# Score and weight blocks of two attention heads: fp32 products on 64 array rows per head in place of split fp32r products on 128 rows, and the second turn of y moved up

## The chip, the cores and the metric

The kernel runs on one core of one Trainium2 chip. The metric is the device time of one execution in microseconds; lower is better. Three executions were timed before the change, and one execution was profiled.

## The reference, cut to what matters

A gated linear attention layer with 64 slots per head, a layer norm, an expert layer and a second layer norm, for 4 batches of 512 tokens of width 512. There are 16 heads. For each head (`q`, `k` 64 wide, `v` 128 wide, `s` 64 slots):

```python
z = cumlogsumexp(s); g = exp(z_prev - z); p = exp(s - z)
hk = hk * g + k_t p_t^T          # step over tokens
ok_t = q_t . hk                  # 64 slots
pv = softmax(ok)
hv = hv * g + p_t v_t^T
ov_t = pv_t . hv                 # 128 wide
o = ov * rsqrt(mean(ov^2) + eps) * g_norm * silu(gate)
out = o @ Wo
```

The kernel computes the recurrences in chunks of 128 tokens. Within a chunk a causal 128x128 block is needed twice for each head: scores (keys times scaled queries, contracted over the head's 64 features), used to sum slots, and weights (the exponentials `e` times `pz`, contracted over the head's 64 slots), used to sum values.

## The kernel before

**Cells.** The attention part is 32 cells: 8 pairs of heads times 4 batches, each with 512 tokens in 4 chunks (`CH`). A cell holds two heads side by side: the 128 partitions of the feature-major tiles `q_t`, `k_t` and `e_t` are 64 rows of one head and 64 rows of the other. The first cell stands ahead of a hardware loop, the loop body has 4 cells, and 3 cells follow it. After the attention comes the expert part (lines from 1091 on), which the change doesn't touch.

**Engines.** The instruction order of each engine is written out by hand, and engines meet at semaphores. TensorE (`cell_tensor`) does, in order: turns (128x128 transposes) of `e` and `k`; the products for v and gate of chunks 0 and 1 (`token_proj`) with the running key sums (`running_keys`); the score blocks; `running_keys(2)`; the turn of `rz`; the turn of half 0 of `y`, the previous cell's output; the slot sums of chunks 0 and 1 into bank `OB`; the turn of half 1 of `y`; the slot sums of chunks 2 and 3; the previous cell's `output_rows`; more v and gate products with `running_values`; the turn of `pz`; the next cell's slot projection; the weight blocks; the next cell's query and key projections; the value products. ScalarE copies banks out and makes the high parts of split numbers, VectorE and GpSimd make the low parts.

**Split products.** A tile is held as high plus low part in type fp32r, and `split_product` (L910) adds three matmuls: high by high, high by low, low by high (L914 to L916). `pair_blocks` (L972) does so for the two blocks of one chunk at once. The left side is the stacked 128 rows of both heads (`lhs_hi`, `lhs_lo`), and the right side is a block-diagonal tile 256 columns wide (`bd_hi`, `bd_lo`), in which each head's 64 rows are filled only in its own 128 columns. Bank `SB[half]` gets chunks 2·half and 2·half+1 of both heads. The parts come from ScalarE (L511, L512, L518, L561, L579, L580), from VectorE (`queries_low` L672, L810 and L812) and from GpSimd (`keys_low` L431, and L445). VectorE then multiplies each bank by the causal mask into `w_t` (`masked`, L683).

**Banks of the turns.** The turned tiles share two PSUM banks, `TB[0]` and `TB[1]`, in the fixed order of L53:

```python
T_USES = ["e", "k", "rz", "y0", "y1", "pz"]
```

They alternate, so `e`, `rz` and `y1` have one bank, and `k`, `y0` and `pz` the other. `turned` (L945) waits, before it writes, until the tile that had the bank before has been read (`wait_read` with `t_read`, L896): `y1` waits for `rz_tok_done`, which ScalarE's copy of the turned `rz` (L558) raises.

Of the kernel before, what the change touches and what calls it, by code (L numbers as in the profile page):

```python
# [11 lines left out]
P = 128  # L12
# [194 lines left out]
def attention(nc, car, x, Wq, Wk, Wv, Wg, Ws, Wo, g_norm, U, V, W1, b1, b2):  # L207
# [10 lines left out]
    with ctx:  # L218
# [26 lines left out]
        bd_hi, bd_lo = sb("bd_hi", [P, 2, T], F32R), sb("bd_lo", [P, 2, T], F32R)  # L245
        lhs_hi, lhs_lo = sb("lhs_hi", [P, T], F32R), sb("lhs_lo", [P, T], F32R)
# [81 lines left out]
        q_lo_done, k_lo_done = sem("q_lo_done"), sem("k_lo_done")  # L328
        e_hi_done, e_lo_done = sem("e_hi_done"), sem("e_lo_done")
# [101 lines left out]
        def keys_low(pool, m):  # L431

            pool.wait_ge(k_done, m.count(1, 1))
            nc.gpsimd.tensor_tensor(lhs_lo[:], k_t[:], lhs_hi[:].bitcast(F32), ALU.subtract).then_inc(k_lo_done, 1)  # L434

        def cell_gpsimd(pool, cell, J=None, last=False):
            if J is not None:

                for i in range(3):
                    split_low(pool, J, i)  # L440
            if last:
                car.norm1_rstd(pool, 0)

            pool.wait_ge(e_hi_done, cell.count(1, 1))
            nc.gpsimd.tensor_tensor(lhs_lo[:], e_t[:, cell.b % 2, :], lhs_hi[:].bitcast(F32),  # L445
                                    ALU.subtract).then_inc(e_lo_done, 1)

            pool.wait_ge(e_tok_hi_done, cell.count(1, 1))
            nc.gpsimd.tensor_tensor(e_tok_lo[:].rearrange("p c (h m) -> p c h m", h=2), e_tok[:, 0:CH - 1, 1:3, :],
                                    e_tok_hi[:].rearrange("p c (h m) -> p c h m", h=2).bitcast(F32),  # L450
                                    ALU.subtract).then_inc(e_tok_lo_done, 1)
            for c in range(CH - 1):
                pool.wait_ge(v_hi_done, cell.count(CH - 1, c + 1))
                nc.gpsimd.tensor_tensor(v_lo[:, c, :], v_tok[:, c, :], v_hi[:, c, :].bitcast(F32),  # L454
                                        ALU.subtract).then_inc(v_lo_done, 1)
            if J is not None:
                for i in range(3, 7):
                    split_low(pool, J, i)
            if not last:
                keys_low(pool, cell.shifted(1))  # L460

            pool.wait_ge(ovar_done, cell.count(1, 1))
            nc.gpsimd.tensor_tensor(orstd[:], ovar[:], minus_half[:], ALU.pow).then_inc(orstd_done, 1)

        @block.gpsimd
        def _(pool):
            pool.wait_ge(own_done, 2)
            nc.gpsimd.affine_select(out=ident[:], in_=ident[:], compare_op=ALU.not_equal, fill=1.0, base=0,
                                    pattern=[[-1, P]], channel_multiplier=1).then_inc(const_done, 1)

            nc.gpsimd.affine_select(out=causal[:], in_=causal[:], compare_op=ALU.is_ge, fill=0.0, base=0,
                                    pattern=[[1, P]], channel_multiplier=-1).then_inc(const_done, 1)
            nc.gpsimd.memset(minus_half[:], -0.5).then_inc(const_done, 1)
            for i in range(7):
                split_low(pool, 0, i)
            pool.wait_ge(const_done, 3)
            keys_low(pool, Cell(None, 0))
            cell_gpsimd(pool, Cell(None, 0))
            with pool.Fori(0, PAIRS - 1) as j:
                for b in range(1, B + 1):  # L480
                    cell_gpsimd(pool, Cell(j, b), j + 1 if b == 3 else None)
            for b in range(1, B):
                cell_gpsimd(pool, Cell(None, B * (PAIRS - 1) + b), last=b == B - 1)
            for kt in range(KT):
                car.w1_low(pool, kt)
# [19 lines left out]
        def queries_scalar(act, m):  # L505
            bk, _ = p_turn(m.shifted(-1), "q")
            ps = PB[bk]
            act.wait_ge(q_proj, m.count(1, 1))
            scale = float(DK) ** -0.5
            nc.scalar.activation(q_t[:], ps[:], ACT.Copy, scale=scale)  # L510
            nc.scalar.activation(bd_hi[0:DK, 0, :], ps[0:DK, :], ACT.Copy, scale=scale)  # L511
            nc.scalar.activation(bd_hi[DK:P, 1, :], ps[DK:P, :], ACT.Copy, scale=scale).then_inc(q_done, 1)  # L512

        def keys_scalar(act, m):
            bk, _ = p_turn(m.shifted(-1), "k")
            act.wait_ge(k_proj, m.count(1, 1))
            nc.scalar.activation(k_t[:], PB[bk][:], ACT.Copy)
            nc.scalar.activation(lhs_hi[:], PB[bk][:], ACT.Copy).then_inc(k_done, 1)  # L518
# [23 lines left out]
        def cell_scalar(act, cell, J=None, wo_J=None, last=False):  # L542
# [17 lines left out]
            act.wait_ge(scores, cell.count(2, 2))  # L560
            nc.scalar.activation(lhs_hi[:], e_t[:, cell.b % 2, :], ACT.Copy).then_inc(e_hi_done, 1)  # L561
# [16 lines left out]
            nc.scalar.activation(pz_t_hi[:].rearrange("p c t -> p (c t)"), TB[bk][:], ACT.Copy)  # L578
            nc.scalar.activation(bd_hi[0:M, 0, :], TB[bk][0:M, :], ACT.Copy)  # L579
            nc.scalar.activation(bd_hi[M:P, 1, :], TB[bk][M:P, :], ACT.Copy).then_inc(pz_t_done, 1)  # L580
# [91 lines left out]
        def queries_low(dve, m):  # L672

            bk, _ = p_turn(m.shifted(-1), "q")
            dve.wait_ge(q_done, m.count(1, 1))
            for h, own_rows in enumerate((slice(0, DK), slice(DK, P))):
                low = nc.vector.scalar_tensor_tensor(out=bd_lo[own_rows, h, :], in0=PB[bk][own_rows, :],
                                                     scalar=float(DK) ** -0.5,
                                                     in1=bd_hi[own_rows, h, :].bitcast(F32), op0=ALU.mult,
                                                     op1=ALU.subtract)  # L680
            low.then_inc(q_lo_done, 1)

        def masked(dve, cell, half, ready, done):  # L683

            dve.wait_ge(ready, cell.count(2, half + 1))
            nc.vector.tensor_tensor(
                w_t[:, 2 * half:2 * half + 2, :, :].rearrange("p c h t -> p (c h) t"),
                SB[half][:].rearrange("p (a t) -> p a t", a=4),
                causal[:].rearrange("p (a t) -> p a t", a=1).broadcast_to([P, 4, P]),
# [56 lines left out]
        def cell_vector(dve, cell, wo_J=None, last=False):  # L746
# [47 lines left out]
            for c in range(CH - 1):  # L794
# [9 lines left out]
                if c == 1:  # L804
# [4 lines left out]
                                            pz_t_hi[:].rearrange("p c t -> p (c t)").bitcast(F32), ALU.subtract)  # L809
                    nc.vector.tensor_tensor(bd_lo[0:M, 0, :], TB[bk][0:M, :], bd_hi[0:M, 0, :].bitcast(F32),  # L810
                                            ALU.subtract)
                    nc.vector.tensor_tensor(bd_lo[M:P, 1, :], TB[bk][M:P, :], bd_hi[M:P, 1, :].bitcast(F32),  # L812
# [15 lines left out]
            if not last:  # L828
                queries_low(dve, nxt)
# [12 lines left out]
        def _(dve):  # L842
# [3 lines left out]
            nc.vector.memset(bd_hi[:].bitcast(F32), 0.0).then_inc(own_done, 1)  # L846
            nc.vector.memset(bd_lo[:].bitcast(F32), 0.0).then_inc(own_done, 1)
            nc.vector.memset(e_tok[:], 0.0).then_inc(own_done, 1)
            dve.wait_ge(own_done, 6)
# [15 lines left out]
            queries_low(dve, m)  # L865
# [6 lines left out]
            dve.wait_ge(own_done, 8)  # L872
# [22 lines left out]
        p_read = {"s": (s_clipped, 1, 2), "q": (q_lo_done, 1, 2), "k": (k_done, 1, 2)}  # L895
# [76 lines left out]
        def pair_blocks(pe, half, done):  # L972

            for c in (2 * half, 2 * half + 1):
                t = tokens(c)
                last = split_product(
                    SB[half][:, (c % 2) * 2 * P:(c % 2 + 1) * 2 * P].rearrange("p (h t) -> p h t", h=2),
                    [((lhs_hi[:, t], lhs_lo[:, t]), (bd_hi[:, :, t], bd_lo[:, :, t]))])
            last.then_inc(done, 1)

        def cell_tensor(pe, cell, last=False):
# [28 lines left out]
            pe.wait_ge(q_lo_done, cell.count(1, 1))  # L1010
            pe.wait_ge(k_lo_done, cell.count(1, 1))
            pair_blocks(pe, 0, scores)
            pair_blocks(pe, 1, scores)
# [3 lines left out]
            if not first(cell):  # L1017
                turned_y(pe, cell, 0)

            for c in range(CH):  # L1020
                if c == 2 and not first(cell):
                    turned_y(pe, cell, 1)
# [4 lines left out]
                pe.wait_ge(scores_masked, cell.count(2, c // 2 + 1))  # L1027
# [36 lines left out]
            pe.wait_ge(pz_lo_done, cell.count(1, 1))  # L1064
            pe.wait_ge(e_lo_done, cell.count(1, 1))
            pair_blocks(pe, 0, weights)
            pair_blocks(pe, 1, weights)
# [9 lines left out]
            for half in range(2):  # L1077
                pe.wait_ge(weights_masked, cell.count(2, half + 1))
# [345 lines left out]
```

## Time and profile before

| what | value |
|---|---|
| median of three timed executions | 1407.0 us (1406.31 to 1410.47) |
| the profiled execution, first to last instruction (span) | 1402.9 us |
| what lies around the span, by the median | 4.1 us |
| TensorE matmul busy | 1370.4 us, 98% |
| VectorE, ScalarE, GpSimd busy | 951.8 us (68%), 567.3 us (40%), 336.4 us (24%) |
| mean granted TensorE clock | 0.998 of full speed |

The profile page gives no execution time of its own beside the span, so the span stands for the profiled execution and 4.1 us is the difference to the median. Matmuls overlap: the time of one in a row is its latency, and what a matmul costs in a stream is the distance from its start to the next one's start. A plain fp32 matmul of the program stands in the trace as two MATMUL records with a weight load (LDWEIGHTS, engine PEld) each. A split product's matmul, or a turn, stands as one.

### The profile page before, as it was taken

What the parts mean: (1) busy time and instruction counts of PE and PEld (TensorE: products, weight loads), DVE (VectorE), ACT (ScalarE), POOL (GpSimd) and SP (SyncE); (2) the same over time, 40 slices, a digit from 0 to 9 for tenths busy, and PEclk for the clock granted to TensorE, in tenths of its full rate; (3) what the DMA queues carried; (4) which work ended last, traced back from release to release, by engine and by line L of the source; (5) the groups of instructions that cost most, each with busy time, mean ns of one, the idle gap of its engine ahead of it and who ended that gap; (6) DMA issues with size and microseconds to landing.
All of it is one profiled execution on the core that took longest, in us unless ns stands there. A gap on an engine that the chain in (4) does not pass through costs nothing. (4 is left out here: it accounts for less than half of the span.)

```text
span 1402.9 us, 21964 instructions
## 1 busy us (share of the span) xinstructions
PE 1370.4 (98%) x7904; PEld 1197.8 (85%) x7904; DVE 951.8 (68%) x1812; ACT 567.3 (40%) x1562; POOL 336.4 (24%) x302
## 2 busy tenths in 40 slices
PE   7999999999999999999999999999999999999998
PEld 6888888888888888888888888888888888878886
DVE  6666776676776677767766776776676767755644
ACT  5344433454344443444334443444344443512210
POOL 3222412233223312331124222331223221210000
PEclk9999999999999999999999999999999999999999
DMA  6000100001000100010001000010000200000000
GB/s 202 9 1 1 51 3 17 0 23 31 16 1 23 30 17 0 2 52 1 16 1 36 17 16 1 23 31 16 1 21 25 61 31 1 1 1 31 30 31 31
DMA packets 35304, 31.78 MB, mean 23 GB/s; under 512 B 7568, under 2 KB 28048, under 8 KB 35216
## 3 DMA queue, kind: packets, MB, share of 16 engines
q1 hardware_dynamic: 35216, 30.44, 7.3%
q8 instruction: 76, 1.25, 0.4%
q14 instruction: 12, 0.10, 0.0%
HBM read 26.24 MB, written 4.19 MB: 22 GB/s over the span
## 5 line engine op out<-in xcount | busy, mean ns | idle before, releaser
L914 PE MATMUL p<-wvg_hi,xt_hi 128*128 128x512 f32 x512 | 210.2, 411 | 0.0
L916 PE MATMUL p<-wvg_hi,xt_lo 128*128 128x512 f32 x512 | 201.2, 393 | 0.0
L915 PE MATMUL p<-wvg_lo,xt_hi 128*128 128x512 f32 x512 | 200.4, 391 | 0.0
L523 ACT ACTIVATE v_tok<-p 128x256 f32<-128x256 f32 x128 | 49.3, 385 | 309.0 <-PE p L916 309.0
L914 PE MATMUL p<-xt_hi,wsqk_hi 128*128 128x512 f32 x384 | 150.5, 392 | 1.4 <-DVE xt_lo L857 1.4
L915 PE MATMUL p<-xt_lo,wsqk_hi 128*128 128x512 f32 x384 | 150.2, 391 | 0.0
L916 PE MATMUL p<-xt_hi,wsqk_lo 128*128 128x512 f32 x384 | 149.4, 389 | 0.0
L454 POOL TENSOR_TENSOR v_lo<-v_tok,v_hi 128x256 fp32r<-128x256 f32 x96 | 84.3, 893 | 195.9 <-ACT v_hi L532 195.9
L434 POOL TENSOR_TENSOR lhs_lo<-k_t,lhs_hi 128x512 fp32r<-128x512 f32 x32 | 41.1, 1284 | 313.3 <-ACT lhs_hi L518 313.3
L916 PEld LDWEIGHTS p<-wvg_hi,xt_lo 128*128 128x128 f32 x512 | 96.3, 188 | 22.5
L915 PEld LDWEIGHTS p<-wvg_lo,xt_hi 128*128 128x128 f32 x512 | 97.0, 190 | 16.7
L914 PEld LDWEIGHTS p<-wvg_hi,xt_hi 128*128 128x128 f32 x512 | 96.8, 189 | 16.2
L670 DVE RECIPROCAL rz_t<-rz_t 128x512 f32<-128x512 f32 x32 | 106.9, 3341 | 0.0
L699 DVE SCALAR_TENSOR_TENSOR gate<-th,p 128x256 f32<-128x256 f32 x128 | 53.9, 421 | 76.0 <-ACT th L527 72.2
L914 PE MATMUL p<-wo_hi,yt_hi 128*128 128x512 f32 x256 | 102.9, 402 | 0.8 <-DVE acc L736 0.5
L916 PE MATMUL p<-wo_hi,yt_lo 128*128 128x512 f32 x256 | 99.9, 390 | 0.0
L915 PE MATMUL p<-wo_lo,yt_hi 128*128 128x512 f32 x256 | 99.7, 389 | 0.0
L445 POOL TENSOR_TENSOR lhs_lo<-e_t,lhs_hi 128x512 fp32r<-128x512 f32 x32 | 40.9, 1277 | 210.4 <-ACT lhs_hi L561 210.4
L736 DVE TENSOR_TENSOR acc<-p,acc 128x512 f32<-128x512 f32 x128 | 87.4, 684 | 1.8 <-PE p L916 1.8
L916 PEld LDWEIGHTS p<-xt_hi,wsqk_lo 128*128 128x128 f32 x384 | 72.1, 188 | 15.5
L914 PEld LDWEIGHTS p<-xt_hi,wsqk_hi 128*128 128x128 f32 x384 | 72.3, 188 | 15.1 <-DVE xt_lo L857 1.8
L915 PEld LDWEIGHTS p<-xt_lo,wsqk_hi 128*128 128x128 f32 x384 | 72.4, 188 | 12.6
(215 smaller groups left out, 3431.1 us busy)
## 6 DMA issues: line engine op xcount, KB each, us to landing
acc<-in_L_attn_hidden_states SPq DMA_DIRECT2D x4, 1024.0 KB, 7.5
raw<-in_L_attn_Wv SPq DMA_DIRECT2D x32, 128.0 KB, 2.4
raw<-in_L_attn_Wg SPq DMA_DIRECT2D x32, 128.0 KB, 2.8
raw<-in_L_attn_Wo SPq DMA_DIRECT2D x16, 256.0 KB, 2.8
out<-acc SPq DMA_DIRECT2D x16, 256.0 KB, 2.3
raw<-in_L_attn_Ws SPq DMA_DIRECT2D x8, 256.0 KB, 2.6
raw<-in_L_attn_Wq SPq DMA_DIRECT2D x8, 256.0 KB, 2.8
raw<-in_L_attn_Wk SPq DMA_DIRECT2D x8, 256.0 KB, 4.6
```

The costliest lines, as they stand in the source:

```text
L434: nc.gpsimd.tensor_tensor(lhs_lo[:], k_t[:], lhs_hi[:].bitcast(F32), ALU.subtract).then_inc(k_lo_done, 1)
L445: nc.gpsimd.tensor_tensor(lhs_lo[:], e_t[:, cell.b % 2, :], lhs_hi[:].bitcast(F32), ALU.subtract).then_inc(e_lo_done, 1)
L454: nc.gpsimd.tensor_tensor(v_lo[:, c, :], v_tok[:, c, :], v_hi[:, c, :].bitcast(F32), ALU.subtract).then_inc(v_lo_done, 1)
L523: nc.scalar.activation(v_tok[:, c, :], PB[bk][:, 0:VW], ACT.Copy).then_inc(v_done, 1)
L670: nc.vector.reciprocal(rz_t[:], rz_t[:]).then_inc(rz_done, 1)
L699: nc.vector.scalar_tensor_tensor(out=gate[:, c, :], in0=th[:, c % 2, :], scalar=1.0, in1=PB[bk][:, VW:2 * VW], op0=ALU.add, op1=ALU.mult). ...
L736: nc.vector.tensor_tensor(a, PB[bk][:], a, ALU.add).then_inc(added, 1)
L914: nc.tensor.matmul(out_, lh, rh, start=(k == 0), stop=False)
L915: nc.tensor.matmul(out_, lh, rl, start=False, stop=False)
L916: last = nc.tensor.matmul(out_, ll, rh, start=False, stop=(k == n - 1))
```

## The change

Both block kinds become plain fp32 products, one per head and chunk, each on its own 64 partitions: rows 0 to 63 for head 0 and 64 to 127 for head 1. Bank `SB[h]` now holds the four chunks of head h, and `head_blocks` goes through the chunks and alternates the heads. All of the `bd` and `lhs` tiles, their copies on ScalarE, their subtractions on VectorE and GpSimd, and two tile clears at the start go. One new fp32 copy of the turned `pz` (`pz_t`) is made ahead of `pz_t_hi`. `masked` handles one head's bank. The slot sums and the value products wait for both masks. The turn of `y` half 1 moves ahead of all slot sums.

```diff
-            act.wait_ge(scores, cell.count(2, 2))
-            nc.scalar.activation(lhs_hi[:], e_t[:, cell.b % 2, :], ACT.Copy).then_inc(e_hi_done, 1)
...
-            nc.scalar.activation(pz_t_hi[:].rearrange("p c t -> p (c t)"), TB[bk][:], ACT.Copy)
-            nc.scalar.activation(bd_hi[0:M, 0, :], TB[bk][0:M, :], ACT.Copy)
-            nc.scalar.activation(bd_hi[M:P, 1, :], TB[bk][M:P, :], ACT.Copy).then_inc(pz_t_done, 1)
+            nc.scalar.activation(pz_t[:], TB[bk][:], ACT.Copy).then_inc(pz_split, 1)
+            nc.scalar.activation(pz_t_hi[:].rearrange("p c t -> p (c t)"), TB[bk][:], ACT.Copy).then_inc(pz_t_done, 1)
...
-        def pair_blocks(pe, half, done):
-
-            for c in (2 * half, 2 * half + 1):
-                t = tokens(c)
-                last = split_product(
-                    SB[half][:, (c % 2) * 2 * P:(c % 2 + 1) * 2 * P].rearrange("p (h t) -> p h t", h=2),
-                    [((lhs_hi[:, t], lhs_lo[:, t]), (bd_hi[:, :, t], bd_lo[:, :, t]))])
-            last.then_inc(done, 1)
+        def head_blocks(keys, queries, done):
+
+            for c in range(CH):
+                t = tokens(c)
+                for h, own_rows in enumerate((slice(0, DK), slice(DK, P))):
+                    mm = nc.tensor.matmul(SB[h][:, t], keys[own_rows, t], queries[own_rows, t],
+                                          start=(c == 0), stop=True, skip_group_check=True)
+                    if c == CH - 1:
+                        mm.then_inc(done, 1)
...
-            pe.wait_ge(q_lo_done, cell.count(1, 1))
-            pe.wait_ge(k_lo_done, cell.count(1, 1))
-            pair_blocks(pe, 0, scores)
-            pair_blocks(pe, 1, scores)
+            head_blocks(k_t, q_t, scores)
...
             if not first(cell):
                 turned_y(pe, cell, 0)
+                turned_y(pe, cell, 1)
 
             for c in range(CH):
-                if c == 2 and not first(cell):
-                    turned_y(pe, cell, 1)
...
-                pe.wait_ge(scores_masked, cell.count(2, c // 2 + 1))
+                pe.wait_ge(scores_masked, cell.count(2, 2))
...
-            pe.wait_ge(pz_lo_done, cell.count(1, 1))
-            pe.wait_ge(e_lo_done, cell.count(1, 1))
-            pair_blocks(pe, 0, weights)
-            pair_blocks(pe, 1, weights)
+            pe.wait_ge(pz_split, cell.count(1, 1))
+            pe.wait_ge(scores_masked, cell.count(2, 2))
+            head_blocks(e, pz_t, weights)
```

The program's instructions for TensorE at the score blocks of a loop cell, before (four groups of three such matmuls stand there; `s` is a bank of `SB`):

```order
L1009 ISA [waits q_done]
L914 MATMUL s<-bd_hi,lhs_hi 128x256 [waits k_lo_done,q_lo_done,y_done]
L915 MATMUL s<-bd_lo,lhs_hi 128x256
L916 MATMUL s<-bd_hi,lhs_lo 128x256
...
L992 REGISTER_ALU
L993 MATMUL xb<-e_tok,k_tok 128x128 [waits hk_kept]
```

The same place now:

```order
L970 ISA [waits q_done]
L937 MATMUL s<-q_t,k_t 128x128 [waits y_done]
L937 MATMUL s<-q_t,k_t 128x128 x7
L953 REGISTER_ALU
L954 MATMUL xb<-e_tok,k_tok 128x128 [waits hk_kept]
```

Twelve matmuls of 256 columns have become eight of 128 columns, and two of the waits are gone.

A few instructions on, TensorE's turns and slot sums, before (`t` is a bank of `TB`, `o` is `OB`):

```order
L950 MATMUL t<-ident,y 128x128 [waits k_tok_done,y_done]
L950 MATMUL t<-ident,y 128x128 x3
L1027 ISA
L1028 MATMUL o<-e_tok,w_t 128x128 [waits scores_masked]
L1030 MATMUL o<-e_tok,w_t 128x128
L1026 MATMUL o<-hk,q_t 128x128 [waits hk_kept]
L1028 MATMUL o<-e_tok,w_t 128x128 [waits scores_masked]
L1030 MATMUL o<-e_tok,w_t 128x128
L950 MATMUL t<-ident,y 128x128 [waits rz_tok_done,y_done]
L950 MATMUL t<-ident,y 128x128 x3
```

and now:

```order
L910 MATMUL t<-ident,rz_t 128x128 x3
L915 REGISTER_ALU
L910 MATMUL t<-ident,y 128x128 [waits k_tok_done,y_done]
L910 MATMUL t<-ident,y 128x128 x3
L910 MATMUL t<-ident,y 128x128 [waits rz_tok_done,y_done]
L910 MATMUL t<-ident,y 128x128 x3
L984 ISA
L985 MATMUL o<-e_tok,w_t 128x128 [waits scores_masked]
L987 MATMUL o<-e_tok,w_t 128x128
```

The turn that waits for `rz_tok_done` stood five slot sums behind the first turn of `y`; now it stands directly behind it.

## Rows read from the trace of the kernel before

**Rows 1.** The page: span, busy time of TensorE and VectorE, granted clock.

```profile
span 1402.9 us, 21964 instructions
PE 1370.4 (98%) x7904; PEld 1197.8 (85%) x7904; DVE 951.8 (68%) x1812; ACT 567.3 (40%) x1562; POOL 336.4 (24%) x302
PEclk9999999999999999999999999999999999999999
```

**Rows 2.** Waits of TensorE: who for whom, us in total, times, longest.

```profile
PE t L950 <- issue: 9.6, 6, 1.8
PE s L1104 <- DMA acc<-in_L_attn_hidden_states: 7.3, 1, 7.3
PE xb L1046 <- POOL v_lo L454: 2.8, 1, 2.8
...
PE s L914 <- DVE bd_lo L812: 0.3, 1, 0.3
```

**Rows 3.** Windows, a cell, its two block passes: us, busy, clock.

```profile
704.49:741.74 37.25, 37.25 (x221) 32.80 (x219) 25.79 (x49) 15.11 (x46) 7.80 (x7) 1.00 0.00 1
710.47:711.88 1.41, 1.41 (x14) 1.41 (x13) 0.93 (x3) 0.66 (x2) 0.00 (x0) 1.00 0.00 0
731.21:732.64 1.43, 1.43 (x13) 1.41 (x12) 0.69 (x1) 0.49 (x1) 0.00 (x0) 1.00 0.00 0
```

**Rows 4.** Timeline from the score blocks to the output rows: start, duration, engine.

```profile
710.47 0.19 PEld L914 LDWEIGHTS s<-bd_hi,lhs_hi 128*128 128x128 f32 x1
...
711.25 0.42 DVE L699 SCALAR_TENSOR_TENSOR gate<-th,p 128x256 f32<-128x256 f32 x1 [0.18 <-ACT th L527]
...
711.58 1.31 DVE L686 TENSOR_TENSOR w_t<-s,causal 128x512 f32<-128x512 f32 x2
...
711.88 0.28 PE L916 MATMUL s<-bd_hi,lhs_lo 128*128 128x256 f32 x1
711.88 0.31 PEld L993 LDWEIGHTS xb<-e_tok,k_tok 128*128 128x128 f32 x2
...
712.12 0.47 PEld L950 LDWEIGHTS t<-ident,rz_t 128*128 128x128 f32 x4
...
712.55 0.47 PEld L950 LDWEIGHTS t<-ident,y 128*128 128x128 f32 x4
...
712.86 0.60 ACT L558 ACTIVATE rz_tok<-t 128x512 f32<-128x512 f32 x1 [1.65 <-PE t L950]
712.99 0.30 PEld L1028 LDWEIGHTS o<-e_tok,w_t 128*128 128x128 f32 x2
713.10 0.39 PE L1028 MATMUL o<-e_tok,w_t 128*128 128x128 f32 x2
713.21 0.30 PEld L1030 LDWEIGHTS o<-e_tok,w_t 128*128 128x128 f32 x2
713.32 0.39 PE L1030 MATMUL o<-e_tok,w_t 128*128 128x128 f32 x2
...
713.87 0.59 ACT L539 ACTIVATE yt_hi<-t 128x512 fp32r<-128x512 f32 x1
...
714.10 0.47 PEld L950 LDWEIGHTS t<-ident,y 128*128 128x128 f32 x4
...
714.50 0.69 DVE L721 TENSOR_TENSOR yt_lo<-t,yt_hi 128x512 fp32r<-128x512 f32 x1 [1.41 <-ACT yt_hi L539]
...
715.88 0.19 PEld L914 LDWEIGHTS p<-wo_hi,yt_hi 128*128 128x128 f32 x1
```

**Rows 5.** Line 558, ScalarE's copy of `rz`: duration min/median/max, first, last; waits.

```profile
L558 ACT ACTIVATE rz_tok<-t x32: 597/597/598, 36.9 to 1201.5; 128x512 f32<-128x512 f32 x32
...
  PE t L950: 54.3, 32
```

**Rows 6.** Timeline of VectorE, then TensorE, around the weight blocks.

```profile
727.93 0.67 DVE L810 TENSOR_TENSOR bd_lo<-t,bd_hi 64x512 fp32r<-64x512 f32 x1
728.62 0.69 DVE L812 TENSOR_TENSOR bd_lo<-t,bd_hi 64x512 fp32r<-64x512 f32 x1
...
733.96 1.26 DVE L686 TENSOR_TENSOR w_t<-s,causal 128x512 f32<-128x512 f32 x2
...
738.13 0.60 PE L1086 MATMUL o<-v_tok,w_t 128*128 128x128 f32 x4
```

More of the change, by code:

```diff
@@ L242, in attention @@
         rz_t = sb("rz_t", [P, T])
-        bd_hi, bd_lo = sb("bd_hi", [P, 2, T], F32R), sb("bd_lo", [P, 2, T], F32R)
-        lhs_hi, lhs_lo = sb("lhs_hi", [P, T], F32R), sb("lhs_lo", [P, T], F32R)
+        pz_t = sb("pz_t", [P, T])
         k_t = sb("k_t", [P, T])
@@ L327, in attention @@
         pz_t_done, pz_lo_done = sem("pz_t_done"), sem("pz_lo_done")
-        q_lo_done, k_lo_done = sem("q_lo_done"), sem("k_lo_done")
-        e_hi_done, e_lo_done = sem("e_hi_done"), sem("e_lo_done")
+        pz_split = sem("pz_split")
         e_tok_hi_done, e_tok_lo_done = sem("e_tok_hi_done"), sem("e_tok_lo_done")
@@ L429, in split_low @@
                                     ALU.subtract).then_inc(w_lo_done, 1)
-        def keys_low(pool, m):
-            pool.wait_ge(k_done, m.count(1, 1))
-            nc.gpsimd.tensor_tensor(lhs_lo[:], k_t[:], lhs_hi[:].bitcast(F32), ALU.subtract).then_inc(k_lo_done, 1)
         def cell_gpsimd(pool, cell, J=None, last=False):
@@ L442, in cell_gpsimd @@
                 car.norm1_rstd(pool, 0)
-            pool.wait_ge(e_hi_done, cell.count(1, 1))
-            nc.gpsimd.tensor_tensor(lhs_lo[:], e_t[:, cell.b % 2, :], lhs_hi[:].bitcast(F32),
-                                    ALU.subtract).then_inc(e_lo_done, 1)
             pool.wait_ge(e_tok_hi_done, cell.count(1, 1))
@@ L458, in cell_gpsimd @@
                     split_low(pool, J, i)
-            if not last:
-                keys_low(pool, cell.shifted(1))
             pool.wait_ge(ovar_done, cell.count(1, 1))
@@ L476, in _ @@
             pool.wait_ge(const_done, 3)
-            keys_low(pool, Cell(None, 0))
             cell_gpsimd(pool, Cell(None, 0))
@@ L509, in queries_scalar @@
             scale = float(DK) ** -0.5
-            nc.scalar.activation(q_t[:], ps[:], ACT.Copy, scale=scale)
-            nc.scalar.activation(bd_hi[0:DK, 0, :], ps[0:DK, :], ACT.Copy, scale=scale)
-            nc.scalar.activation(bd_hi[DK:P, 1, :], ps[DK:P, :], ACT.Copy, scale=scale).then_inc(q_done, 1)
+            nc.scalar.activation(q_t[:], ps[:], ACT.Copy, scale=scale).then_inc(q_done, 1)
         def keys_scalar(act, m):
@@ L516, in keys_scalar @@
             act.wait_ge(k_proj, m.count(1, 1))
-            nc.scalar.activation(k_t[:], PB[bk][:], ACT.Copy)
-            nc.scalar.activation(lhs_hi[:], PB[bk][:], ACT.Copy).then_inc(k_done, 1)
+            nc.scalar.activation(k_t[:], PB[bk][:], ACT.Copy).then_inc(k_done, 1)
         def values_scalar(act, cell, c):
@@ L670, in inverse_vector, with masked @@
             nc.vector.reciprocal(rz_t[:], rz_t[:]).then_inc(rz_done, 1)
[L672 to L685, printed above, removed]
+        def masked(dve, cell, h, ready, done):
+            dve.wait_ge(ready, cell.count(2, h + 1))
             nc.vector.tensor_tensor(
-                w_t[:, 2 * half:2 * half + 2, :, :].rearrange("p c h t -> p (c h) t"),
-                SB[half][:].rearrange("p (a t) -> p a t", a=4),
-                causal[:].rearrange("p (a t) -> p a t", a=1).broadcast_to([P, 4, P]),
+                w_t[:, :, h, :],
+                SB[h][:].rearrange("p (c t) -> p c t", c=CH),
+                causal[:].rearrange("p (a t) -> p a t", a=1).broadcast_to([P, CH, P]),
                 ALU.mult).then_inc(done, 1)
@@ L808, in cell_vector @@
                     nc.vector.tensor_tensor(pz_t_lo[:].rearrange("p c t -> p (c t)"), TB[bk][:],
[L809 to L812, printed above, removed]
+                                            pz_t_hi[:].rearrange("p c t -> p (c t)").bitcast(F32),
                                             ALU.subtract).then_inc(pz_lo_done, 1)
@@ L827, in cell_vector @@
                 inverse_vector(dve, nxt)
-            if not last:
-                queries_low(dve, nxt)
             if wo_J is not None:
@@ L845, in _ @@
             nc.vector.memset(own[:], 0.0).then_inc(own_done, 1)
-            nc.vector.memset(bd_hi[:].bitcast(F32), 0.0).then_inc(own_done, 1)
-            nc.vector.memset(bd_lo[:].bitcast(F32), 0.0).then_inc(own_done, 1)
             nc.vector.memset(e_tok[:], 0.0).then_inc(own_done, 1)
-            dve.wait_ge(own_done, 6)
+            dve.wait_ge(own_done, 4)
             nc.vector.memset(own[0:M, 0, :], 1.0).then_inc(own_done, 1)
@@ L864, in _ @@
             sums_vector(dve, m)
-            queries_low(dve, m)
             x_low(2)
@@ L871, in _ @@
             dve.wait_ge(const_done, 2)
-            dve.wait_ge(own_done, 8)
+            dve.wait_ge(own_done, 6)
             cell_vector(dve, m)
@@ L890, in _ @@
                 add_rows(dve, tail, c)
-        p_read = {"s": (s_clipped, 1, 2), "q": (q_lo_done, 1, 2), "k": (k_done, 1, 2)}
+        p_read = {"s": (s_clipped, 1, 2), "q": (q_done, 1, 2), "k": (k_done, 1, 2)}
         t_read = {"e": (e_tok_done, 1, 1), "k": (k_tok_done, 1, 1), "rz": (rz_tok_done, 1, 1), "pz": (pz_lo_done, 1, 1)}
@@ L1077, in cell_tensor @@
             for half in range(2):
-                pe.wait_ge(weights_masked, cell.count(2, half + 1))
+                pe.wait_ge(weights_masked, cell.count(2, 2))
                 for c in (2 * half, 2 * half + 1):
```

## The prediction

> **What bounds the kernel now.** I read the page first. TensorE is busy 98% of a span of 1402.9 us at full clock, VectorE 68% [rows 1], so any time of another engine counts only where TensorE waits for it. The waits of TensorE come next: they are few and small, the largest being 9.6 us at six loop turns and 7.3 us for the first load, and the low parts that the change removes made it wait 0.3 us, once [rows 2]. So the relief of ScalarE, VectorE and GpSimd is worth about nothing: the 1.36 us that VectorE spends in L810 and L812 in a cell [rows 6], the copies, and GpSimd's two subtractions end ahead of TensorE's need. The cover is the products that TensorE runs meanwhile. The windows then say what can be won: a cell takes 37.25 us, its score blocks 1.41 us and its weight blocks 1.43 us [rows 3]. Over 32 cells both kinds are 32 x 2.84 = 91 us. The timeline of one cell gives the rest [rows 4].
>
> **The blocks.** A plain fp32 product of 128 columns is already in the trace: the slot sums L1028 and L1030, each two records. They start at 713.10 and 713.32, 0.22 us apart, with all 128 rows in use [rows 4]. After the change a block pass is eight such products on 64 rows each. No row of before shows a matmul on half the rows, so the price is bounded from both sides:
> - One after the other, as full-row products go now: 8 x 0.222 = 1.78 us, 0.36 us more than the mean 1.42 us of now.
> - The two heads side by side, since they use different rows and different banks: 4 x 0.222 = 0.89 us at best. Each product is two records, and if matmuls start in program order, head 1's first record starts with head 0's second, so the last head's pair ends half a product (0.11 us) later: 1.00 us.
> - The edges, where TensorE goes from 128 rows to 64 and back. At nothing they are as the present changes from one form to another. At worst the array empties first: a matmul record of 0.28 us (the L916 at 711.88) must then end before the next load, which takes 0.11 us from its start to the matmul's (712.99 to 713.10) [rows 4], where now loads lie under matmuls. That adds up to about 0.28 us per edge, 0.55 us per pass.
>
> I take side by side at 1.00 us, with small edges. The operands of the two heads share no partition, no weight and no bank, and alternate in program order, and TensorE's loads already run beside its matmuls: at 711.88 a load and a matmul start together [rows 4]. A pass then gains 0.42 us: 64 x 0.42 = 27 us.
>
> The Trainium skill speaks for this: "TensorE: Matmul & The Clock Gate", Part 3 on row and column tiling, says that matmuls on different row groups start about 4 ns apart and run together. By it the pass would come to about what I take. Neither of its examples is fp32 with 128 columns, and no row here shows it.
>
> **The turn of y.** Here the change adds a wait. The turned `rz` and half 1 of `y` share a bank, so this turn waits for ScalarE's copy L558. That copy starts at 712.86, 0.74 us after the first load of the `rz` turn at 712.12, and takes 0.60 us [rows 4], in every cell alike: 597 to 598 ns in 32 cells, and ScalarE was idle before it and waited for TensorE each time [rows 5], so it can't start sooner. The bank is free 1.34 us behind the `rz` turn's start. VectorE's L721 starts 0.04 us behind the end of ScalarE's L539 (713.87 + 0.59 = 714.46, 714.50) [rows 4], so I add 0.04 us: 1.38 us. Before, the turn came at 714.10, 1.98 us behind, and waited for nothing. Now it is due behind the turn of `rz` (712.12 to 712.55) and that of `y` half 0 (712.55 to 712.99), 0.87 us behind. It is late by 1.38 - 0.87 = 0.51 us. Behind it on TensorE stand all slot sums and then the output rows, so nothing hides it. 31 cells have a `y` before them: 31 x 0.51 = 16 us. The stall doesn't depend on how fast the blocks are, since both its ends hang on the `rz` turn. Bounds: 0.40 us a cell if the signal comes before the copy's last 0.1 us, 0.60 us if TensorE restarts slowly: 12 to 19 us.
>
> **The masks.** The slot sums now wait for both. With a pass of 1.00 us the blocks end at 711.47; VectorE's gate product ends at 711.67 (711.25 + 0.42), and the two masks, 1.31 us together, run to 712.98 [rows 4]. TensorE has then done `running_keys(2)` (0.24 us), `rz` (0.43), `y` half 0 (0.44), the stall (0.51) and `y` half 1 (0.44): 711.47 + 2.06 = 713.53. The masks are 0.5 us early, covered by the stall; without it they would be just in time. If blocks run one after the other, VectorE's masks start as the last products land, about 712.5, and end near 713.8, and TensorE comes at 714.3: also hidden. At the weight blocks the masks end 3 us before TensorE's first value product (735.22 and 738.13) [rows 6]. They stand behind VectorE's scan of the next cell's exponentials, not behind the blocks' speed, so a gain of 0.4 us there is covered.
>
> **The sum.** Blocks -27 us, turn of `y` +16 us, all else 0: -11 us. The span goes from 1402.9 to about 1392 us, and with the 4.1 us that lie around it the median from 1407.0 to about **1396 us**. Per cell: the score part, from the first score load to the output rows (5.41 us now, 710.47 to 715.88 [rows 4]), gets no shorter, 5.41 - 0.41 + 0.51 = 5.51 us; the weight part gets 0.43 us shorter.
>
> **The rivals.** Each is worked out from 1407.0 us.
> - *One after the other.* If the weight loads of both heads, or the columns, pass one at a time, each pass costs 1.78 us: 64 x 0.36 = 23 us, plus 16 us: 1446 us, slower. It decides above a pass of 1.17 us, where 64 x 0.25 eats the 16 us. For it: the slot sums' loads also stand 0.22 us apart per product (712.99, 713.21) [rows 4], so loads may be what paces them now, and halving rows does not halve a load. Against it: the loads of two heads fill different rows.
> - *Side by side, but the edges cost.* Emptying the array at both edges in full gives 1.00 + 0.55 = 1.55 us a pass: 64 x 0.13 = 8, plus 16: 1431 us. Half of that, 1.27 us, gives 64 x (-0.15) + 16 = +6: 1413 us. For it: nothing in the trace mixes 64 and 128 rows, so nothing excludes it.
> - *The stall is hidden.* If ScalarE's copy were free earlier, -27 alone: 1380 us. Rows 5 leave this little room.
> - *Nothing moves.* Two gains and losses cancel, 1403 to 1411 us; a pass between 1.10 and 1.24 us does it.
>
> The Trainium skill has a rule against the change: "TensorEngine Tiling (Array Packing)", Key Properties, says that a change of tiling mode drains TensorE, though a change of tile does not. There are two such changes in a pass. By that rule the edges' rival holds at least in part; no row here shows its size. "TensorE: Matmul & The Clock Gate", LDWEIGHTS, adds that a load's time goes by its columns alone, 107 ns for 128, which is what the serial rival needs if loads do not run side by side.
>
> **How the numbers follow.** Side by side with a pass of 0.89 to 1.10 us: 0.48, giving 1389 to 1403 us (its own range is 1385 to 1406 with the stall's bounds). Pass of 1.10 to 1.24 us: 0.12. Edges or partial overlap beyond that, up to 1.6 us: 0.12, 1411 to 1435 us. One after the other: 0.26, 1440 to 1450 us. Stall hidden: 0.02. I give 1386 to 1447 us, which leaves out 0.02 below and about 0.13 above. A measurement of this kernel tells about 0.3%, 4.2 us, from no change. Faster 0.50, same 0.12, slower 0.38.
>
> **What would show it.** In the changed trace: a window over a block pass of about 1.0 us (1.8 if serial, 1.3 to 1.6 if edges cost), and starts of head 1's records on top of head 0's. Gaps around the first record of a pass show the edges. TensorE's waits should have a new one, L910 on ScalarE's rz copy, 31 times 0.3 to 0.5 us (idle time looks shorter than the lost time, since the record of the matmul before reaches into it). The weight masks should still end before the value products. The prediction is wrong if a pass is not near 1.0 us, or if the turn of `y` doesn't wait.

## The result and the profile after

The changed kernel takes 1416.4 us (median of four, 1414.7 to 1419.8) against 1406.9 us: 1.0074 times the time before, 95% interval 1.0056 to 1.0092. Measured again beside other kernels it took 1413.9 us, ratio 1.0041 (1.0026 to 1.0055). It is slower by 0.4 to 0.7%, where the prediction said 1396 us and faster.

The page after, its span and its busy times:

```profile
span 1418.1 us, 22055 instructions
PE 1373.8 (97%) x8160; PEld 1174.3 (83%) x8160; DVE 864.5 (61%) x1682; ACT 482.5 (34%) x1402; POOL 254.6 (18%) x238
```

The groups by line and form of the changed kernel, the two of the new products (busy us, mean ns, idle):

```profile
L937 PE MATMUL s<-q_t,k_t 64*128 64x128 f32 x512 | 37.2, 285 | 0.0
L937 PE MATMUL s<-pz_t,e_t 64*128 64x128 f32 x512 | 37.2, 285 | 0.0
```

VectorE lost 87 us of work, ScalarE 85 and GpSimd 82 against [rows 1], and the time still went up: none of them bounds. Each kind's 32 passes fill 37.2 us, 1.16 us a pass of 16 records. In the slot sums of [rows 4] a product's two records take 0.22 us, 0.11 us each; 16 such starts one after the other would need 1.65 us from the first start to the last alone, so records of the two heads lie on top of each other. TensorE's waits (for whom, total us, times, longest) against [rows 2]:

```profile
PE t L910 <- issue: 11.2, 6, 2.0
PE t L910 <- ACT rz_tok L540: 10.6, 31, 0.3
```

The predicted wait of the `y` turn is there, 31 times. The timeline of one cell, beside [rows 4]:

```profile
719.37 0.41 PEld L954 LDWEIGHTS xb<-e_tok,k_tok 128*128 128x128 f32 x2
719.59 0.38 PE L954 MATMUL xb<-e_tok,k_tok 128*128 128x128 f32 x2
...
719.90 0.97 PEld L937 LDWEIGHTS s<-q_t,k_t 64*128 64x128 f32 x16
719.91 1.16 PE L937 MATMUL s<-q_t,k_t 64*128 64x128 f32 x16
...
721.00 0.30 PEld L954 LDWEIGHTS xb<-e_tok,k_tok 128*128 128x128 f32 x2
...
721.10 1.29 DVE L654 TENSOR_TENSOR w_t<-s,causal 128x512 f32<-128x512 f32 x2 [0.20 <-PE s L937]
721.21 0.47 PEld L910 LDWEIGHTS t<-ident,rz_t 128*128 128x128 f32 x4
721.32 0.60 PE L910 MATMUL t<-ident,rz_t 128*128 128x128 f32 x4
721.65 0.47 PEld L910 LDWEIGHTS t<-ident,y 128*128 128x128 f32 x4
721.76 0.60 PE L910 MATMUL t<-ident,y 128*128 128x128 f32 x4
721.96 0.60 ACT L540 ACTIVATE rz_tok<-t 128x512 f32<-128x512 f32 x1 [1.51 <-PE t L910]
...
722.67 0.42 PEld L910 LDWEIGHTS t<-ident,y 128*128 128x128 f32 x4 [0.55 <-issue]
722.70 0.63 PE L910 MATMUL t<-ident,y 128*128 128x128 f32 x4 [0.34 <-ACT rz_tok L540]
...
725.51 0.19 PEld L874 LDWEIGHTS p<-wo_hi,yt_hi 128*128 128x128 f32 x1
```

Three things are to be read here. First, the 16 records of a pass, eight products, take 1.10 us from the first load to the next full-row load (719.90 to 721.00): the heads do run side by side. Second, the load ahead of the pass is late. From the load of `running_keys(1)` to the first load of the score blocks it was 0.34 us before (710.13 to 710.47), and is 0.53 us now (719.37 to 719.90). Third, the second `y` turn follows the first by 0.94 us (721.76 to 722.70) in place of 0.44, a loss of 0.50 us. From the first score load to the output rows it takes 5.61 us (719.90 to 725.51); it was 5.41 [rows 4], and 5.51 was forecast.

The low clock is the fourth. The first of the six turns of the program's loop, on TensorE:

```profile
216.42 0.65 PE L910 MATMUL t<-ident,e_t 128*128 128x128 f32 x4 [1.95 <-issue]
```

Windows of 10 us around four of the six turns (length, busy times, granted clock; DMA stands last):

```profile
210.00:220.00 10.00, 8.05 (x47) 7.09 (x46) 5.70 (x12) 5.18 (x21) 1.64 (x1) 0.86 0.20 57
365.00:375.00 10.00, 8.09 (x46) 7.08 (x45) 4.41 (x12) 5.18 (x21) 1.64 (x1) 0.83 0.19 56
...
825.00:835.00 10.00, 8.05 (x37) 6.67 (x36) 3.38 (x12) 3.62 (x18) 1.64 (x1) 0.83 0.20 54
980.00:990.00 10.00, 8.74 (x38) 7.26 (x40) 2.98 (x12) 2.60 (x9) 1.64 (x1) 0.83 0.16 45
```

At each of them TensorE sits idle for about 1.9 us at the loop's turn, and behind it the clock was at its lower level, 1.2 GHz, for a few us; 0.83 over 10 us is 1.7 us lost (the first stretch runs past the end of its window). The third turn had 1.53 us of idle time and the fourth 1.89 us, and both kept the full clock. The profile before shows 1.00 from 50 us to 1390 us, here at its first turn:

```profile
210.00:220.00 10.00, 8.17 (x52) 7.15 (x51) 5.88 (x15) 5.73 (x24) 2.93 (x2) 1.00 0.19 56
```

In this profiled execution the low clock is some 7 us of the 15.2 us between the two spans. Another 1.6 us is idle time at the loop's turns, 11.2 us in place of 9.6.

### The profile page after: what moved, and what is told of

Its sections match the earlier page's. It is cut to its first block and busy times, and to the rows that moved or that the text cites. A ratio compares the mean times of both kernels' runs of the same rounds, so it can differ in the third digit from the quotient of the medians.

```text
span 1418.1 us, 22055 instructions
## 1 busy us (share of the span) xinstructions
PE 1373.8 (97%) x8160; PEld 1174.3 (83%) x8160; DVE 864.5 (61%) x1682; ACT 482.5 (34%) x1402; POOL 254.6 (18%) x238
## 5 line engine op out<-in xcount | busy, mean ns | idle before, releaser
L874 PE MATMUL p<-xt_hi,wsqk_hi 128*128 128x512 f32 x384 | 154.3, 402 | 1.4 <-DVE xt_lo L818 1.4
L449 POOL TENSOR_TENSOR orstd<-ovar,minus_half 128x8 f32<-128x8 f32 x32 | 52.4, 1637 | 423.0 <-DVE ovar L801 423.0
L438 POOL TENSOR_TENSOR e_tok_lo<-e_tok,e_tok_hi 128x384 fp32r<-128x384 f32 x32 | 32.6, 1018 | 323.0 <-ACT e_tok_hi L547 323.0
L654 DVE TENSOR_TENSOR w_t<-s,causal 128x512 f32<-128x512 f32 x128 | 81.6, 679 | 6.5 <-PE s L937 6.5
L876 PEld LDWEIGHTS p<-xt_hi,wsqk_lo 128*128 128x128 f32 x384 | 72.4, 188 | 15.7
```

The costliest lines, as they stand in the source:

```text
L654: nc.vector.tensor_tensor(w_t[:, :, h, :], SB[h][:].rearrange("p (c t) -> p c t", c=CH), causal[:].rearrange("p (a t) -> p a t", a=1).broa ...
L874: nc.tensor.matmul(out_, lh, rh, start=(k == 0), stop=False)
L876: last = nc.tensor.matmul(out_, ll, rh, start=False, stop=(k == n - 1))
```

## The experiments

Theory A: a block pass is a little shorter than before, because the heads run side by side and its two edges, the changes between 128 and 64 rows, eat most of that; the loss is the new wait of the `y` turn. Rival B: the half-row passes themselves bring the loss, by their edges and by a lower clock, and the wait is replaced by another one if it is removed.

**1. Half 1 of y in a bank of its own.** The turn goes into the product bank of the gate of chunk 1, which is free by then and is next written by the output rows of chunk 1. The turn leaves the order of the `TB` banks, and all output rows but those of chunk 0 wait until this half has been read.

```diff
-        return uses
+        return [u for u in uses if u != "y1"]
...
+            if half == 0 or (cell.j is None and cell.b == CELLS):
+                turned(pe, cell, f"y{half}", blocks, y_turned)
+                return
+            pe.wait_ge(gate_done, cell.count(CH, 2))
+            for i, blk in enumerate(blocks):
+                last = nc.tensor.transpose(y_bank(cell, half)[:, i * P:(i + 1) * P], blk, ident[:])
+            last.then_inc(y_turned, 1)
...
-            pe.wait_ge(yt_lo_done, prev.count(2, c // 2 + 1))
+            pe.wait_ge(yt_lo_done, prev.count(2, 1 if c == 0 else 2))
```

> The changed kernel, with half 1 of y turned into the product bank that the gate of chunk 1 has just left, so that this turn no longer waits for the copy of rz. Theory A (the added wait of the y turn is the loss, a block pass is 0.14 us shorter than before with its edges): the wait goes, 31 x 0.50 = 15.5 us; the masks are then just in time, so about 1416.4 - 15.5 = 1401, and 3 to 5 us less if the low-clock stretches go with the wait: 1396 to 1401 us. Rival B (the half-row passes bring the loss, by their edges and by lowering the clock): the wait of 0.5 us is replaced by a wait for the masks or by nothing, and the low-clock stretches stay: 1405 to 1412 us.

Measured: 1395.4 us, 0.9919 (0.9902 to 0.9935) of the kernel before. The timeline of a cell shows the turn (L927, into a bank `p`) 0.44 us behind the first:

```profile
744.75 1.29 DVE L660 TENSOR_TENSOR w_t<-s,causal 128x512 f32<-128x512 f32 x2 [0.19 <-PE s L949]
...
744.98 0.60 PE L915 MATMUL t<-ident,rz_t 128*128 128x128 f32 x4
...
745.41 0.60 PE L915 MATMUL t<-ident,y 128*128 128x128 f32 x4
...
745.85 0.60 PE L927 MATMUL p<-ident,y 128*128 128x128 f32 x4
...
746.29 0.39 PE L997 MATMUL o<-e_tok,w_t 128*128 128x128 f32 x2
```

Nothing takes the wait's place: the masks end at 746.04, just ahead of the first slot sum, and the sums start in stride. This time no low clock appears at a loop turn (mean clock 0.998), though TensorE sat idle for 1.93 and 2.00 us at two of them. B falls for the waits. Without the wait the blocks are a gain.

**2. The kernel before, with the turn of y moved up and nothing else.**

```diff
                 turned_y(pe, cell, 0)
+                turned_y(pe, cell, 1)
 
             for c in range(CH):
-                if c == 2 and not first(cell):
-                    turned_y(pe, cell, 1)
```

> The kernel before, with one move alone: the turn of y half 1 stands directly behind that of half 0. Theory A: it waits 0.5 us for the copy of rz in 31 cells, 1406.9 + 15.5 = 1422 us, and if the wait brings low-clock stretches a few us more. Rival B: the wait is cheap where blocks are split products (masks and sums as before), at most 1412 us, and no new low-clock stretch.

Measured: 1421.8 us, 1.0111 (1.0086 to 1.0136), 15 us over the kernel before. Its waits have the same line as the changed kernel's:

```profile
PE t L950 <- ACT rz_tok L558: 10.6, 31, 0.3
```

The move costs 15 us by itself, with no half-row product in the program. The mean clock was 0.998 or more in three of its four runs and 0.996 in the other, so the waits of half a microsecond don't bring the low clock.

**3. The weight blocks alone.** The weights' operands and masks go with them; score blocks, masks of the scores and turns of `y` are as before.

```diff
...
-            pair_blocks(pe, 0, weights)
-            pair_blocks(pe, 1, weights)
+            head_blocks(e, pz_t, weights)
...
```

> The kernel before, with the weight blocks alone as fp32 products per head on 64 rows (their operand pz_t lies in the tile of k_t, which is free then); score blocks, their masks and the turns of y stay as before. Theory A: 32 passes, each 0.14 us shorter: 1406.9 - 4.5 = 1402.4 us, no new low-clock stretch. Rival B (half-row passes lower the clock or cost as much as before): 1407 to 1412 us.

Measured: 1402.1 us, 0.9964 (0.9951 to 0.9977), 4.7 us less than the kernel before measured beside it (1406.8 us): 0.15 us for each of 32 passes, as A has it; the interval allows 0.10 to 0.22 us. The weight pass between its full-row neighbours, before:

```profile
731.00 0.39 PE L916 MATMUL p<-xt_hi,wsqk_lo 128*128 128x512 f32 x1
...
732.66 0.40 PE L914 MATMUL p<-xt_hi,wsqk_hi 128*128 128x512 f32 x1
...
732.89 0.40 PE L915 MATMUL p<-xt_lo,wsqk_hi 128*128 128x512 f32 x1
```

and in this experiment:

```profile
730.48 0.39 PE L915 MATMUL p<-xt_hi,wsqk_lo 128*128 128x512 f32 x1
730.80 1.16 PE L985 MATMUL s<-k_t,e_t 64*128 64x128 f32 x16
731.89 0.50 PE L913 MATMUL p<-xt_hi,wsqk_hi 128*128 128x512 f32 x1
732.23 0.39 PE L914 MATMUL p<-xt_lo,wsqk_hi 128*128 128x512 f32 x1
```

From the last neighbour ahead to the second behind it took 1.89 us (731.00 to 732.89) and takes 1.75 us (730.48 to 732.23), 0.14 us less. Two starts 0.23 us apart and 0.89 us of products would make 1.35 us, so the two edges cost 0.40 us.

**4. Two more edges.** The full-row `running_keys(2)` stands in the middle of the score blocks: `head_blocks` calls it between chunks 1 and 2.

```diff
+                if c == 2 and amid is not None:
+                    amid()
...
-            head_blocks(k_t, q_t, scores)
-            running_keys(2)
+            head_blocks(k_t, q_t, scores, lambda: running_keys(2))
```

> The changed kernel, with the full-row matmul running_keys(2) moved from behind the score blocks into their middle, between chunks 1 and 2: two more changes between 128 and 64 rows in each of 32 cells, the same instructions otherwise. Theory A (an edge costs 0.20 us): 64 x 0.20 = 13 us more than the changed kernel, about 1429 us. Rival (the gaps at a pass come from something else, such as its semaphore waits or the change of bank): the same as the changed kernel, 1416 us.

Measured: 1423.6 us, 1.0127 (1.0103 to 1.0151). The timeline:

```profile
720.22 0.38 PE L956 MATMUL xb<-e_tok,k_tok 128*128 128x128 f32 x2
...
720.53 0.71 PE L939 MATMUL s<-q_t,k_t 64*128 64x128 f32 x8
721.17 0.49 PE L956 MATMUL xb<-e_tok,k_tok 128*128 128x128 f32 x2
...
721.59 0.72 PE L939 MATMUL s<-q_t,k_t 64*128 64x128 f32 x8
722.24 0.66 PE L910 MATMUL t<-ident,rz_t 128*128 128x128 f32 x4
722.73 0.60 PE L910 MATMUL t<-ident,y 128*128 128x128 f32 x4
```

From `running_keys(1)` to the first turn of `y` it takes 2.51 us (720.22 to 722.73), in the changed kernel 2.17 (719.59 to 721.76). Two more edges for the same instructions cost 0.34 us, 0.17 us each; 32 x 0.34 = 11 us. Against the changed kernel's 1413.9 to 1416.4 us it is 7 to 10 us more by the medians. At the same mean clock, 0.998, three runs of this version took 1423.2 to 1424.0 us and the one of the changed kernel 1411.9 us, 11 to 12 us more. The direction and the timeline are as A said; the size of 13 us was a little high, as the edge was taken at 0.20 us.

**5. Every score pass twice.**

```diff
-                    if c == CH - 1:
+                    if c == CH - 1 and done is not None:
...
+            head_blocks(k_t, q_t, None)
             head_blocks(k_t, q_t, scores)
```

> The changed kernel with every score pass done twice in a row, the second writing the same blocks over the first: 32 times 16 more half-row records with no additional change between 64 and 128 rows. Theory A (a pass is 0.89 us of products plus 0.4 us of edges): 32 x 0.89 = 28.5 us more than the changed kernel, about 1442 us, and the starts of the 16 pairs run on without a gap between the two passes. Rival (the loss per pass lies in the half-row products themselves, 1.29 us each time): 32 x 1.29 = 41 us more, about 1455 us.

Measured: 1442.7 us (two runs, 1438.6 and 1446.8), 1.0249 (1.0121 to 1.0377). The interval is too wide to exclude the rival's 1455 us by the total; the timeline decides. A pass of 32 records:

```profile
734.40 2.06 PE L937 MATMUL s<-q_t,k_t 64*128 64x128 f32 x32
```

2.06 us for 32 records against 1.16 for 16: eight products more cost 0.90 us. Four pairs at 0.22 us are 0.89, so the two heads overlap in full, and what is left of a pass belongs to its two edges and not to the products: the rival had 1.29 us for the second eight.

**6. One head after the other.** The two loops of a pass are swapped.

```diff
-            for c in range(CH):
-                t = tokens(c)
-                for h, own_rows in enumerate((slice(0, DK), slice(DK, P))):
+            for h, own_rows in enumerate((slice(0, DK), slice(DK, P))):
+                for c in range(CH):
+                    t = tokens(c)
```

> The changed kernel with the loops of a block pass swapped: the four products of head 0, then the four of head 1, so that neighbours in program order use the same rows. Theory (side by side needs alternation, because matmuls start in program order): only the seam between the heads overlaps, a pass takes about 0.2 us of edges plus 15 starts 0.11 us apart, 1.8 to 2.0 us in place of 1.29: 32 to 45 us more, 1448 to 1461 us. Rival (the hardware finds the other head's products further back in its queue, or the gain has nothing to do with neighbours): within 5 us of the changed kernel, 1416 us.

Measured: 1449.1 us (one run). A pass of the weights:

```profile
718.34 1.71 PE L937 MATMUL s<-pz_t,e_t 64*128 64x128 f32 x16
```

1.71 us in place of 1.16, times 64 is 35 us, and the one run is 35 us above the changed kernel's 1413.9: alternation in program order is needed for the full overlap. But 16 starts one after the other, 0.11 us apart, would take 1.65 us from first to last and some 0.28 more to the end, and this pass is shorter than that by 0.2 us: head 1 starts ahead of head 0's last records. The size was at the low end of the expectation.

**7. The turn of y back between the sums.** Blocks and masks stay changed.

```diff
                 turned_y(pe, cell, 0)
-                turned_y(pe, cell, 1)
 
             for c in range(CH):
+                if c == 2 and not first(cell):
+                    turned_y(pe, cell, 1)
```

> The changed kernel with the turn of y half 1 put back between the slot sums of chunks 1 and 2; blocks and masks stay changed. Theory A: the wait for the copy of rz (0.50 us) goes, and a shorter wait for the two masks takes its place, since they end some 0.25 us after the turn of y half 0: 31 x 0.25 = 8 us less than the changed kernel, 1404 to 1409 us. Rival (the move was needed: without it the masks cost as much as the copy of rz does): 1414 to 1418 us.

Measured: 1412.0 us, 1.0023 (1.0012 to 1.0034), only 2 us less than the changed kernel on the same chip. The expectation of 1404 to 1409 us missed. The timeline:

```profile
717.53 1.29 DVE L654 TENSOR_TENSOR w_t<-s,causal 128x512 f32<-128x512 f32 x2 [0.20 <-PE s L937]
...
718.19 0.60 PE L910 MATMUL t<-ident,y 128*128 128x128 f32 x4
...
718.87 0.30 PEld L986 LDWEIGHTS o<-e_tok,w_t 128*128 128x128 f32 x2 [0.32 <-DVE w_t L654]
...
719.20 0.39 PE L988 MATMUL o<-e_tok,w_t 128*128 128x128 f32 x2
```

The masks run to 718.82, so the first sum's load comes at 718.87 where 718.51 was its turn, 0.35 us late and not 0.25: 31 x 0.15 = 5 us of gain. The low clock takes some of that back: it came behind three of the six loop turns in the profiled execution, and the mean clock was 0.995 or less in six of the ten runs, in one of seven of the changed kernel beside it. At the same mean clock, 0.997, the two runs of this version took 1408.3 and 1409.3 us and the three of the changed kernel 1412.2 to 1414.1 us, about 4.5 us more, as the timeline has it. So the masks need the move's cover, and the move needs a bank that is free: only experiment 1 has both.

**8. The changed kernel and experiment 1 once more.**

> The changed kernel once more, for the low-clock stretches at the turns of the program's loop. If they belong to this kernel, most runs show a mean clock of 0.993 to 0.996 and 1415 to 1420 us again. If they come by chance at loop turns of any of these kernels, the runs spread between about 1411 us (mean clock 0.998) and 1420 us (0.993), and the time goes with the clock.

> The version with half 1 of y in a product bank once more, beside the changed kernel on the same chip: 1395 us and 0.992 of the kernel before, if the first measurement holds; 20 us less than the changed kernel, of which 15.5 us are the wait and the rest the low-clock stretches, if these come again in the other.

Measured: 1413.9 us (1411.9 to 1416.1, mean clock 0.998 to 0.995) and 1398.1 us (1396.2 to 1400.8, 0.997 to 0.993; ratio 0.9933, 0.9917 to 0.995). The gap is 15.7 us here, the wait's 15.5 us almost exactly, and not the 20 us expected with the low clock as frequent as at first. The second reading of the first expectation holds in the main: with the two measurements together, runs of the changed kernel go from 1411.9 us at 0.998 to 1419.8 us at 0.993, and the kernel before shows the same, 1402.5 us at 0.999 to 1412.2 us at 0.995. The traces show a low clock behind loop turns in both versions: four times and once in the two executions of the changed kernel, not at all and once in those of experiment 1. For the kernel before only the mean clocks of its runs speak of it, since its one trace has none at a turn. The low clock isn't particular to the changed kernel; whether it comes equally often in all versions is not shown. In this measurement 4 of 18 runs of the kernel before had a mean clock of 0.995 or less, against 6 of 10 in experiment 7.

## Why the prediction was wrong

- **What bounds the kernel**: right. Three engines lost over 80 us of work each, and only TensorE's order counted.
- **The blocks, side by side**: right, and better than taken. Eight products cost 0.89 us: the half product by which I had the last head end later (1.00 us) isn't there, as experiment 5 and the 1.16 us for 16 records show.
- **The edges**: here the prediction failed, at the term of its sum for the change between 128 and 64 rows. It took them "as the present changes from one form to another", at nothing, with 0.28 us each as the bound. They cost 0.17 to 0.20 us each, 0.4 us a pass, 25 us in all, which leaves 0.14 us of gain a pass: 0.84 us per cell was forecast for both kinds, about 0.29 us came. The pass with its edges is 1.28 us, within 0.01 of the half-price case in the rivals (1.27 us, 1413 us), to which I had given little. "TensorEngine Tiling (Array Packing)", Key Properties, of the Trainium skill, which I set against the change, says that a change of tiling mode drains TensorE. Experiment 4 agrees that each change costs time and gives the size, 0.17 us, less than the 0.28 us worked out for emptying in full; that the array empties is not shown, since the ends of matmuls in the trace are modelled.
- **The turn of y**: right in mechanism and size. 0.51 us forecast, 0.50 us in the trace, and alone it costs 15 us (experiment 2), 16 forecast.
- **The masks**: right that they are covered behind the stall, and just in time without it where the turn of `y` stays ahead of the sums (experiment 1).
- **The sum**: with the edge at its price, 64 x (-0.14) + 31 x 0.50 = +6.5 us, or 1413.5 us. Two errors of opposite sign made the forecast less wrong than the edges alone: they add 25 us to its 1396, and the products at 0.89 in place of 1.00 us take 7 off, 1414 us. The timeline has the rise too: a cell takes 37.50 us (first value product at 710.11 and 747.61), 0.25 us more than the 37.25 of [rows 3], where the terms give 0.22. The second measurement is 6.4 us above the kernel before. The 3 us more of the first fit the low clock behind loop turns, of which the prediction had none. Why the first four runs had more of it stays open; the later runs show it comes and goes.

The value products that bound a cell of the changed kernel:

```profile
710.11 0.60 PE L1042 MATMUL o<-v_tok,w_t 128*128 128x128 f32 x4
...
747.61 0.60 PE L1042 MATMUL o<-v_tok,w_t 128*128 128x128 f32 x4
```

## What to carry to other kernels

Here half-row products of two heads side by side ran at double the rate of products one after the other, but each change between full and half rows cost as much as one and a half to two full-row records: make the runs of half-row work long, or count the edges first. When an instruction is moved up, ask which buffer it writes and who reads that buffer last; here the wait cost 15 us, and another bank, free at that point, took it away. A move that gives one wait its cover can be a new wait: price both, and test each half of the change alone. The version of experiment 1 is 0.7 to 0.8% faster than the kernel before.

## What the runs showed of the hardware

- A pair of half-row fp32 records, one per head, costs 0.11 us (16 more records took 0.90 us in experiment 5), as one full-row record does; with the heads one after the other in program order a pass took 1.71 us, less than 16 starts in a row would (experiment 6).
- A change between 128 and 64 rows costs 0.17 to 0.20 us, taken as half of a pair: 0.34 us for two more in experiment 4, 0.40 us for the two of a weight pass in experiment 3. The way in alone is 0.19 us in the changed kernel (0.53 us from load to load in place of 0.34).
- TensorE's clock dropped to 1.2 GHz behind a loop turn with about 1.9 us of idle time in some executions and not in others, at 1.7 us each; turns with 1.93 and 2.00 us of idle time kept the full clock in experiment 1, so the length of the idle time alone doesn't decide. 31 waits of 0.5 us did not bring it about (experiment 2).
